# Key products written in order and read with a stride, bn_aggr for the statistics of the tail, and later reads on GpSimd

## What is computed

```python
x = layernorm(x + retention(x, W_Q, W_K, W_V, W_G, W_O, gn))      # decayed linear attention, 8 heads
x = layernorm(x + ternary_ffn(x, w1, w2, h1, h2, w3))             # 256 -> 1024 -> 1024 -> 1024 -> 256
x = layernorm(x + scan(x, W_k, W_v, W_q))                         # see below
x = layernorm(x + channel_mix(x, W_r, W_k, W_v, mu_r, mu_k))      # token shift, sigmoid gate, relu^2

def step(S, kvq):            # scan over the FIRST axis (4 steps); S is [position, 32 blocks, 8, 8]
    k_norm = k_t / (norm(k_t) + 1e-06)
    delta = v_t - einsum('bnij,bnj->bni', S, k_norm)
    S_new = tanh(S + einsum('bni,bnj->bnij', delta, k_norm))
    Sq = einsum('bnij,bnj->bni', S_new, q_t)
    return S_new, Sq * silu(Sq)
```

## Time and profile before

| | |
|---|---|
| median of 3 runs | 1132.73 us (1132.68 to 1133.84) |
| the profiled execution | 1132.0 us, its span from first to last instruction 1130.1 us |
| mean granted TensorE clock | 0.996 of full speed |
| busy over the span | TensorE 1097.6 us (97%), VectorE 944.7 (84%), ScalarE 592.3 (52%), GpSimd 512.2 (45%) |

### The profile page before, as it was taken

The page is one execution under the profiler, slowest core; times in us unless marked ns, Lnnn a source line. Parts: engine busy times, 40 slices in busy tenths (PEclk is TensorE's granted clock), DMA queues, the critical chain, the costliest instruction groups (busy, mean ns, idle before and its releaser), DMA issues.

```text
span 1130.1 us, 16851 instructions
## 1 busy us (share of the span) xinstructions
PE 1097.6 (97%) x5925; PEld 855.1 (76%) x5925; DVE 944.7 (84%) x1415; ACT 592.3 (52%) x988; POOL 512.2 (45%) x426
## 2 busy tenths in 40 slices
PE   9999999999999999999999999999999999999786
PEld 4566666678787777878778877878787788778575
DVE  4788888973034998999899889989998998899898
ACT  2345555555435355645655574556456555754544
POOL 1466677676333244324433432443244334364653
PEclk9999999999999999999999999999999999999899
DMA  7346555623531440423132323404231323231001
GB/s 262 109 158 246 205 202 201 247 100 112 168 112 49 139 130 19 130 80 127 56 113 83 123 74 111 148 19 124 81 128 51 116 78 108 75 112 57 1 1 40
DMA packets 45131, 127.03 MB, mean 112 GB/s; under 512 B 4368, under 2 KB 21520, under 8 KB 43152
## 3 DMA queue, kind: packets, MB, share of 16 engines
q1 hardware_dynamic: 43920, 114.20, 30.3%
q10 hardware_dynamic: 1152, 12.07, 2.9%
HBM read 117.86 MB, written 19.92 MB: 122 GB/s over the span
## 4 chain that ended last, share of the span: by engine, by line
PE 73%; DVE 16%; POOL 4%; issue 3%; ACT 2%; DMA 0%; SPq 0%; POOLq 0%; DVEq 0%; ACTq 0%
PE lower L1243 43%; PE bank L1243 17%; PE lower L440 5%; PE lower L572 2%; POOL state L748 2%; POOL rgn L757 2%; PE bank L1232 1%; DVE tmp L2290 1%; DVE tmp L2276 1%; PE bank L487 1%; DVE Sq L2278 1%; DVE tmp L2301 1%; DVE y L847 1%; DVE delta L2297 1%; DVE S L2303 1%
## 5 line engine op out<-in xcount | busy, mean ns | idle before, releaser
L2059 POOL TENSOR_TENSOR a_lo<-whole,a_hi 128x512 fp32r<-128x512 f32 x128 | 181.6, 1435 | 260.3 <-ACT a_hi L1644 172.4
L1243 PE MATMUL lower<-b_hi,ring 128*128 128x512 f32 x512 | 193.8, 396 | 1.4 <-ACT a_hi L1644 1.4
L1243 PE MATMUL lower<-b_lo,ring 128*128 128x512 f32 x512 | 190.9, 391 | 1.7 <-POOL b_lo L2059 1.7
L1243 PE MATMUL lower<-a_hi,ring 128*128 128x512 f32 x496 | 187.5, 394 | 0.0
L1243 PE MATMUL lower<-a_lo,ring 128*128 128x512 f32 x496 | 185.4, 390 | 0.0
L2059 POOL TENSOR_TENSOR b_lo<-whole,b_hi 128x512 fp32r<-128x512 f32 x64 | 93.5, 1469 | 144.4 <-ACT b_hi L1644 125.8
L1627 ACT ACTIVATE S<-S 128x1024 f32<-128x1024 f32 x56 | 58.6, 1059 | 172.8 <-DVE S L2303 168.9
L1643 ACT ACTIVATE whole<-lower,hs 128x512 f32<-128x512 f32 x126 | 86.2, 685 | 81.0 <-PE lower L1243 79.2
L1243 PEld LDWEIGHTS lower<-b_hi,ring 128*128 128x128 f32 x512 | 96.2, 188 | 21.9 <-issue 1.8
L1243 PEld LDWEIGHTS lower<-b_lo,ring 128*128 128x128 f32 x512 | 96.1, 188 | 21.9 <-POOL b_lo L2059 2.3
L440 PE MATMUL lower<-wa,xT 128*128 128x512 f32 x240 | 109.3, 599 | 2.1 <-DVE turned L817 1.4
(11 more groups left out here) (293 smaller groups left out, 2418.8 us busy)
## 6 DMA issues: line engine op xcount, KB each, us to landing
ring<-ffn_copy_dram SPq DMA_DIRECT2D x128, 512.0 KB, 3.5
look<-ffn_dram ACTq DMA_DIRECT2D x6, 1879.0 KB, 6.9
ffn_copy_dram<-ffn_dram SPq DMA_DIRECT2D x4, 2112.0 KB, 9.7
rope<-rope_dram SPq DMA_DIRECT2D x8, 512.0 KB, 8.0
xtok<-x_dram SPq DMA_DIRECT2D x8, 512.0 KB, 4.1
x1in<-x_dram SPq DMA_DIRECT2D x8, 512.0 KB, 4.8
x1res<-x_dram SPq DMA_DIRECT2D x8, 512.0 KB, 3.1
xT<-xT_dram SPq DMA_DIRECT2D x7, 512.0 KB, 8.3
```

The costliest lines, as they stand in the source:

```text
L1243: ins = nc.tensor.matmul(out, a, b, start=(first and n == 0), stop=(last and n == len(pairs) - 1))
L2059: nc.gpsimd.tensor_tensor(lo[:, m, :], t["whole"][:, m % 4, :], hi[:, m, :].bitcast(F32), ALU.subtract).then_inc(lo_done, 1)
```

## The change

Three things. `times` is laid out [half, block, i, j], in the order of the state: VectorE writes it in order, and TensorE reads slice j with 8 values between neighbours. `row_moments` gets its statistics from columns of its own (`end_stats`, one place for each use) and forms mean and variance with one `bn_aggr` a row, then negates the mean (not for the final group, whose last step subtracts now) and adds epsilon; `earlier_moments` uses it too. `read_q(s, hf)` of steps 0 and 1 waits for the second half's `times_key`.

```diff
+        end_stats = sb(top, "end_stats", [P, 5 * BATCH, 6])
-        def row_stats(steps, r, rows):
-            for b in rows:
-                ins = nc.vector.bn_stats(out=stats[:, b, :], in_=r[:, b, :])
+        def row_stats(steps, r, rows, st=None):
+            for n, b in enumerate(rows):
+                ins = nc.vector.bn_stats(out=stats[:, b, :] if st is None else st[:, n, :], in_=r[:, b, :])
             steps.done(ins)
-        def row_moments(steps, mv, rows, ve_ready):
+        def row_moments(steps, mv, rows, ve_ready, st, negated=True):
             steps.wait()
-            st, sp, m = stats[:, rows], spread[:, rows], mv[:, rows]
-            nc.vector.tensor_tensor(m[:, :, 0], st[:, :, 1], st[:, :, 4], ALU.add)
-            nc.vector.tensor_tensor(sp, st[:, :, 1], st[:, :, 4], ALU.subtract)
-            steps.done(nc.vector.tensor_tensor(m[:, :, 1], st[:, :, 2], st[:, :, 5], ALU.add))
+            for n, b in enumerate(range(rows.start, rows.stop)):
+                ins = nc.vector.bn_aggr(out=mv[:, b, :], in_=st[:, n, :])
+            steps.done(ins)
             steps.wait()
-            nc.vector.tensor_scalar(m[:, :, 0], m[:, :, 0], -0.5, None, ALU.mult)
-            nc.vector.tensor_tensor(sp, sp, sp, ALU.mult)
-            steps.done(nc.vector.tensor_scalar(m[:, :, 1], m[:, :, 1], 1.0 / DIM, EPS, ALU.mult, ALU.add))
-            steps.wait()
-            nc.vector.scalar_tensor_tensor(out=m[:, :, 1], in0=sp, scalar=0.25, in1=m[:, :, 1],
-                                           op0=ALU.mult, op1=ALU.add).then_inc(ve_ready, 1)
+            if negated:
+                nc.vector.tensor_scalar(mv[:, rows, 0], mv[:, rows, 0], -1.0, None, ALU.mult)
+            nc.vector.tensor_scalar(mv[:, rows, 1], mv[:, rows, 1], EPS, None, ALU.add).then_inc(ve_ready, 1)
...
-            tn["times"] = sb(ctx, "times", [P, 2, BS, HALF * BS])
+            tn["times"] = sb(ctx, "times", [P, 2, HALF, BS, BS])
...
-                        product(tensor_delta(hf), [(ident[:], x) for x in (v, *(t["times"][:, hf, j, :] for j in range(BS)))]
+                        product(tensor_delta(hf).rearrange("p (n i) -> p n i", i=BS),
+                                [(ident[:], x) for x in (v.rearrange("p (n i) -> p n i", i=BS),
+                                                         *(t["times"][:, hf, :, :, j] for j in range(BS)))]
                                 ).then_inc(fin_delta, 1)
...
-                            pool.wait_ge(fin_times_k, step_of(s, hf))
+                            pool.wait_ge(fin_times_k, step_of(s, 1 if s in (0, 1) else hf))
...
                     def earlier_moments():
-                        moments(ln3, x3, t["mv3"], ve3)
-                        ln3.end()
+                        st = end_stats[:, 2 * BATCH:3 * BATCH]
+                        ln3.wait()
+                        row_stats(ln3, x3, range(BATCH), st)
+                        row_moments(ln3, t["mv3"], slice(0, BATCH), ve3, st)
...
-                            w = t["times"][:, hf].rearrange("p j (n i) -> p n i j", i=BS)
+                            w = t["times"][:, hf]
...
-                                                       ALU.add, ALU.mult)
+                                                       ALU.subtract, ALU.mult)
```

More of the change, by code:

```diff
@@ L991, in build @@
             tw["mixw"] = tw["ffn"][:, COL_W1:COL_W1 + KD * HID].rearrange("p (k w n) -> p k w n", k=KD, n=DIM)
-            tw["times"] = tw["ffn"][:, COL_W2:COL_W2 + KD * HID].rearrange("p (h j n) -> p h j n", h=2, j=BS)
+            tw["times"] = tw["ffn"][:, COL_W2:COL_W2 + KD * HID].rearrange("p (h n i j) -> p h n i j", h=2, i=BS, j=BS)
         with ExitStack() as ctx:
@@ L2496, in ffn_row @@
                         after("x2", b)
-                        row_stats(fin, x2, range(b, b + 1))
+                        row_stats(fin, x2, range(b, b + 1), end_stats[:, b:b + 1])
                     def x2_moments(rows):
-                        row_moments(fin, t["mv2"], rows, ve2)
+                        row_moments(fin, t["mv2"], rows, ve2, end_stats[:, rows])
                     def guess_of(rows):
@@ L2613, in x3_moments @@
                         after("x3", g)
-                        row_stats(fin, x3, range(rows.start, rows.stop))
-                        row_moments(fin, t["mv3"], rows, ve3)
+                        st = end_stats[:, BATCH + rows.start:BATCH + rows.stop]
+                        row_stats(fin, x3, range(rows.start, rows.stop), st)
+                        row_moments(fin, t["mv3"], rows, ve3, st, g < FINAL)
                     def normed_by_hand(g, r, mv, rstd, rooted, count):
@@ L2643, in end_moments @@
                         dve.wait_ge(left_y4, g + 1)
-                        row_stats(fin, left_result(t, g), range(rows.start, rows.stop))
-                        row_moments(fin, left_moments(t, g)[0], rows, ve4)
+                        at = (3 + LEFT[g][0] - d) * BATCH
+                        st = end_stats[:, at + rows.start:at + rows.stop]
+                        row_stats(fin, left_result(t, g), range(rows.start, rows.stop), st)
+                        row_moments(fin, left_moments(t, g)[0], rows, ve4, st, g < FINAL)
                     tail.begin(d)
```

## The result

| | median | runs | profiled execution, its span |
|---|---|---|---|
| before | 1133.13 us | 18 | 1132.0, 1130.1 us |
| after | 1135.07 us | 18 | 1134.2, 1132.4 us |

The changed kernel is slower: ratio 1.0018, 95% interval 1.001 to 1.0025, some 2 us. Forecast was 4.1 us faster, 1128.6 us, counted from the 1132.73 us of the first three runs; the 18 runs put the kernel before at 1133.13.

What follows compares the result with a forecast made beforehand. VectorE's own order was taken to bound the tail after 1044 us. Key products 2.6 plus statistics 1.7 minus later reads 0.2 gave 4.1 us off the 1132.73 us median: 1128.6 us, range 1127.3 to 1133.4.

Steps and rivals of the forecast that it cites:

- The place and the order of work: Tail after 1044 us: VectorE's own order sets the time up to the last LayerNorm row; TensorE would be late next.
- the cover: Steps 1 and 2: TensorE's deltas ready when VectorE reaches outer(1,0), outer(1,1), outer(2,0), with 0.1 to 0.4 us to spare.
- VectorE's writes: Key products into `times`, steps 1 and 2: in-order writes save 0.645 us each, four times, 2.6 us.
- TensorE's strided read, taken as free: Delta sums reading `times` 32 bytes apart: no extra cost taken, records staying at about 0.11 us; called the weakest step.
- the upper bound of 0.08 us a record: TensorE's read of `times`: extra cost from VectorE's scattered write, 0.63 ns an element, 1.3 us a delta.
- its first rival: TensorE's strided read costs about what VectorE's scattered write did, 0.08 us a record: 0.6 us off, 1132.1 us, chance 0.22.
- The range: Whole kernel: 1127.3 to 1133.4 us, taking in the first rival up to twice a record's time.
- the second rival: TensorE's strided record costs three times its time or over: 1139 us, chance 0.08; a loss from about twice 0.11 us.
- The statistics: `row_moments` with bn_aggr at 0.12 us each: 1.7 us saved, 2.3 with 0.07 us each.
- The later reads: GpSimd's read_q(0,0) and read_q(1,0) waiting for the second half's product: 0.2 us charged, bounds 0 and 0.4.
- The guard: When times_key(1,1) waits for tanh(1,1), later reads avoid holding the two-operand product for up to 2.3 us.
- The sum: Whole change: 2.6 + 1.7 - 0.2 = 4.1 us off, 1128.6 us; better end 4.9 us off (1127.8).

Runs made afterwards that it cites:

- the pairs: Changed kernel with `times` in groups of two values of j, TensorE reading 8 bytes apart, against the kernel before: 1128.18 us, ratio 0.9955.
- late reads: GpSimd's reads released by the second half's product, as in the change; the pairs with them: 1128.18 us, ratio 0.9955 to the kernel before.
- a kernel made for it: Pairs with ScalarE's gate tanh of group 0 put ahead of tanh(1,1): reads released by first half 1129.91 us (0.9972), by second half 1128.22 us (0.9958).
- early reads: GpSimd's reads released by the first half's product, as before the change; the pairs and statistics with them: ratio 0.997 to the kernel before.

## Why the prediction was wrong, point by point

**The place and the order of work**: right. VectorE set the time of the tail before, and what would be late next was named as TensorE, with 0.1 to 0.4 us to spare ahead of the three outer products. Those three are where it waited. In the profiled execution of the pairs with late reads, where TensorE's read costs nothing, the cover held: VectorE had no wait for TensorE ahead of any of the three.

**VectorE's writes**: right. 2.6 us forecast; the first pair went from 3.57 to 2.36 us from its start to the next instruction's, and all four last 1.22 us.

**TensorE's strided read, taken as free**: this is the step that failed. The sum put nothing for it; it cost 0.12 us a record, 1.94 us a delta sum, more than the upper bound of 0.08 us a record taken from VectorE's scattered write. The bound was carried over per element from an engine that spends 1.1 ns on an element in order (2.28 us for 2048) to one that spends 0.86 (0.11 us for 128). Neither the extra time an element nor the factor carried over: VectorE's scattered pair took 1.6 times as long as one in order, TensorE's record 2.1 times. Setting the term to nothing because the nearest row was far was a choice without a row behind it, while the rule that the prediction quotes from the Trainium skill spoke for a cost, and the prediction had the outcome of that as its first rival, at 1132.1 us with a chance of 0.22. With 0.12 instead of 0.08 us a record the rival's own sum gives, for three delta sums in a row, 16 x 0.04 x 3 = 1.9 us more than its 0.6 off: 1.3 slower, and 2.0 was measured. The rest is the stretch from delta(2,1) on, which the rival left out: there the fourth sum takes TensorE through the products of group 2 without the 1.09 us that it idled behind them before, and the path of the last stores with it. The rival counted 1.4 us won between outer(2,0) and the end (0.65, 0.34 and 0.38), and 0.7 came: outer(2,0) is 2.57 us late, the pair of last stores starts 1.89 us late. Before and after:

```profile
1126.12 1.93 SPq L1211 DMA_DIRECT2D out_dram<-x2res  x2
```

```profile
1128.01 2.24 SPq L1208 DMA_DIRECT2D out_dram<-x2res  x2
```

The range, up to 1133.4 us, was too narrow for the same reason: it ended at twice a record's time and counted three sums. The remark in the second rival, that the change becomes a loss where a record takes about twice its 0.11 us or more, came true.

**The statistics**: the mechanism right, the size a little low. A first bn_aggr is followed by its dependent after 0.22 us and each further one costs 0.07, not 0.12. One row takes 0.35 us (1045.69 to 1046.04) instead of 0.73, four take 0.64 (1064.40 to 1065.04) instead of 0.78. Alone the part gave 2.6 us, with an interval from 1.6 to 3.7; 1.7 was forecast, 2.3 with the lower price. The 0.25 us for group 2 came as forecast: its two bn_aggr take the time of any two, although a read of GpSimd is under way.

```profile
1097.33 0.25 DVE L198 BATCH_NORM_AGGREGATE mv<-end_stats 128x2 f32<-128x6 f32 x2
```

```profile
1095.04 2.69 POOL L2144 TENSOR_TENSOR x1in<-whole,kvq 128x1024 f32<-128x1024 f32 x1 [8.82 <-DVE times L2543]
```

**The later reads**: right. The reads are released after the second product and take their own time, step 1's 2.36 us instead of the 3.77 it showed when it started beside VectorE's second product:

```profile
1069.51 2.35 POOL L2144 TENSOR_TENSOR x1in<-whole,kvq 128x1024 f32<-128x1024 f32 x1 [2.74 <-ACT kvq L1832]
...
1081.55 2.36 POOL L2144 TENSOR_TENSOR x1in<-whole,kvq 128x1024 f32<-128x1024 f32 x1 [2.51 <-DVE times L2543]
```

The products of step 0 start 0.81 us earlier than before (1067.00 against 1067.81), `times_key(1, 0)` 0.63 (1078.97 against 1079.60): 0.18 us lost on the way, with GpSimd's key root between them; 0.2 was charged. The guard, which the prediction named without a number in the sum, is shown above in a kernel made for it.

**The sum**: with a read that costs nothing (the pairs) the whole change gives 5.1 us (3.5 to 6.7 by its interval), where 4.1 was forecast for that case with 4.9 as its better end. The terms other than the read were sound.

## What to carry to other kernels

When a layout is turned round to spare one engine a scattered access, price the scattered access that the other engine gets, and look for a layout between the two: here runs of two fp32 values serve the writer and the reader at full rate, and turn a loss of 0.18% into a gain of 0.45%. A cost for which the trace has no row is not zero; where a rule of the Trainium skill speaks for one and the next engine has no slack, it belongs in the likeliest case. A wait that looks useless in one profile can be a guard against an execution in which an operand comes late; the spread of several executions shows it, a single profile doesn't.

## What the runs showed of the hardware

TensorE's fp32 record of 128 columns took 0.111, 0.113, 0.229 and 0.232 us with 4, 8, 16 and 32 bytes between its reads: one step by a factor of two between 8 and 16 bytes. VectorE's product of 1024 values took 1.22 us in runs of 8 bytes, 16 bytes or in order, and 1.93 us when each value lay 512 bytes from the last. A product of VectorE with two operands in SBUF that started during a read of GpSimd lasted 2.36 instead of 1.22 us, and reads that started beside such products lasted 3.2 to 3.9 instead of 2.35 us. TensorE's granted clock around 1070 us differed between the traces. In the stretch from 1070 to 1075 us it was 1.00 in three and 0.50 to 0.68 in the other eleven, behind a wait for ScalarE of 1.8 to 3.0 us that ended between 1065 and 1068 us. The nine traces with a clock of 1.00 from 1050 to 1060 us all had the dip here; of the five with 0.70 to 0.83 there two had it from 1070 to 1075, one only from 1066 to 1070 (0.57), and two had none. No run shows what decides it. In the pairs TensorE's gate products of group 0 ended at 1079.3 with the dip and late reads, at 1076.9 without it and early reads; 0.4 us of that reached VectorE.
